# Cross-attention and gated feed-forward on one core: weight loads moved to SP's ring, first rows of maxima to ACT's, normalisation of q and additions of epsilon to POOL

## The reference

```python
q = (x - mean(x, -1)) / sqrt(var(x, -1) + 1e-5)
for head h (16 rows of q and of ctx):
    s = q_h.T @ ctx_h * 16 ** -0.5            # 256 x 256
    att_h = ctx_h @ softmax(s, -1).T          # 16 x 256
x = x + gamma * att
n = layernorm(x)
out0 = gelu(n @ W0a.T + b0a) @ W0b.T + b0b    # 256 -> 512 -> 256
out1 = relu(n @ W1a.T + b1a) @ W1b.T + b1b
x = x + (out0 if argmax(softmax(n @ Wg.T)) == 0 else out1)
```

## Time and profile before

| what | us |
|---|---|
| median of 3 runs | 257.08 (255.61 to 258.86) |
| the profiled execution | 256.82 |
| its span, first to last instruction | 255.0 |
| PE busy with matmuls | 221.7 (87% of the span) |
| DVE busy | 170.5 (67%) |
| ACT busy | 143.6 (56%) |
| POOL busy | 97.0 (38%) |
| POOL's power of 128x1 (L241), mean of 31 | 0.592 |

### The profile page before, as it was taken

The page is one execution under the profiler, slowest core; times in us unless marked ns, Lnnn a source line. Parts: engine busy times, 40 slices in busy tenths (PEclk is TensorE's granted clock), DMA queues, the critical chain, the costliest instruction groups (busy, mean ns, idle before and its releaser), DMA issues.

```text
span 255.0 us, 5113 instructions
## 1 busy us (share of the span) xinstructions
PE 221.7 (87%) x1968; PEld 171.4 (67%) x1968; DVE 170.5 (67%) x354; ACT 143.6 (56%) x216; POOL 97.0 (38%) x126
## 2 busy tenths in 40 slices
PE   0567926888898999999999999999999999899994
PEld 0434513444476879787878887888778687778883
DVE  2777565698986798878878886988597534523302
ACT  2012323467568748874878488758854986532220
POOL 5492230133794842293239224822441145001000
PEclk9999999959799999999999999999999999999999
DMA  4498999884934448266917691758202000000101
GB/s 165 67 182 143 253 196 186 260 121 114 137 93 85 131 82 186 44 164 84 196 21 178 92 182 18 146 101 123 50 20 64 3 23 3 21 23 0 41 0 42
DMA packets 19563, 25.75 MB, mean 101 GB/s; under 512 B 2644, under 2 KB 13140, under 8 KB 19284
## 3 DMA queue, kind: packets, MB, share of 16 engines
q1 hardware_dynamic: 18024, 22.15, 44.7%
q10 hardware_dynamic: 1516, 3.29, 5.1%
HBM read 11.28 MB, written 2.10 MB: 52 GB/s over the span
## 4 chain that ended last, share of the span: by engine, by line
PE 71%; DVE 10%; ACT 8%; DMA 5%; issue 4%; POOL 0%; DVEq 0%; ACTq 0%
PE ff L769 17%; PE od L712 9%; PE ff L790 9%; PE st L700 9%; PE ff L796 5%; PE ff L808 5%; PE smax L688 5%; ACT P L538 4%; DMA qkst<-mlow 3%; PE od L720 3%; DVE nmax L375 3%; PE st L675 2%; ACT hid L578 2%; PE od L727 2%; DVE nmax L368 2%
## 5 line engine op out<-in xcount | busy, mean ns | idle before, releaser
L538 ACT ACTIVATE P<-st 128x1024 f32<-128x1024 f32 x64 | 65.7, 1027 | 58.4 <-PE st L700 49.9
L375 DVE TENSOR_REDUCE nmax<-smax 128x4 f32<-128x1024 f32 x54 | 66.1, 1225 | 28.5 <-PE smax L688 28.1
L241 POOL TENSOR_TENSOR mv<-mv,power 128x1 f32<-128x1 f32 x31 | 18.4, 592 | 73.7 <-DVE mv L340 73.7
L700 PE MATMUL st<-qkst 50*128 50x256 f32 x240 | 31.3, 340 | 13.2 <-ACT P L538 6.7
L769 PE MATMUL ff<-xnTh,w1h 128*128 128x256 f32 x128 | 37.5, 293 | 1.2 <-DVE y L446 1.2
L700 PEld LDWEIGHTS st<-qkst 50*128 50x128 f32 x240 | 18.7, 193 | 27.9 <-ACT P L538 10.2
L578 ACT ACTIVATE hid<-ff,b1t 128x256 f32<-128x256 f32 x64 | 26.8, 471 | 16.7 <-PE ff L769 16.5
L769 PE MATMUL ff<-xnTh,w1l 128*128 128x256 f32 x128 | 36.0, 281 | 0.0
L769 PE MATMUL ff<-xnTl,w1h 128*128 128x256 f32 x128 | 35.9, 281 | 0.0
L265 POOL TENSOR_TENSOR hidL<-hid,hidH 128x1024 fp32r<-128x1024 f32 x12 | 28.6, 2387 | 18.5 <-DVE hidH L435 14.1
L712 PE MATMUL od<-P,vt 128*32 128x256 f32 x512 | 35.5, 424 | 0.0
(11 more groups left out here) (84 smaller groups left out, 353.4 us busy)
## 6 DMA issues: line engine op xcount, KB each, us to landing
qkst<-parts SPq DMA_DIRECT2D x87, 128.0 KB, 4.5
xv<-in_xv SPq DMA_DIRECT2D x16, 256.0 KB, 3.0
qk<-in_qk SPq DMA_DIRECT2D x15, 256.0 KB, 4.0
out<-y SPq DMA_DIRECT2D x16, 128.0 KB, 2.4
w1t<-in_w ACTq DMA_DIRECT2D x1, 1024.0 KB, 10.0
w2t<-in_w ACTq DMA_DIRECT2D x1, 1024.0 KB, 9.0
qkst<-parts ACTq DMA_DIRECT2D x3, 128.0 KB, 6.3
qk<-in_first SPq DMA_DIRECT2D x1, 256.0 KB, 3.9
```

The lines of the kernel that those rows point to most:

```text
L241: pool.tensor_tensor(mv[:, b % 2, 11:12], mv[:, b % 2, 10:11], power[:, 0:1], ALU.pow).then_inc(s_rstd, 1)
L375: dve.tensor_reduce(nmax[:, c % 2, :, :, j].rearrange("p a e -> p e a"), (ff if c in WIDE and j % 2 else smax)[:, :, :, :], AX.X, ALU.max, ...
L538: act.activation(P[:, b % 2, j, :, :, :].rearrange("p e a l -> p (e a l)"), st[:, :, :, :].rearrange("p e a l -> p (e a l)"), ACT.Exp, sca ...
L700: mm = pe.matmul(st[:, e, a, :], qkst[rows, s, j, 1, a * 128:(a + 1) * 128], qkst[rows, s, j, 0, :], start=True, stop=True)
```

## The change

- SP: of the DMAs at the start, `stacks(2)` and `load_qk(4)` come ahead of `load_xv(0)`, and `load_xv(1)` and `load_qk(5)` come behind `stacks(3)`; in b = 1 `load_qk(6)` comes behind `stacks(4)`. `w1t` is loaded by SP at the end of b = 1, `w2t` at the end of b = 2; before, ACT issued them in slots 0 and 4.
- The rows of maxima of samples 1 to 3 are issued by ACT, in its ring, behind `copy_max`; those of samples 4 to 15 stay with SP.
- `q_norm` for samples 2 to 15 runs on POOL, directly behind `rstd`; that of samples 0 and 1 stays on DVE.
- The addition of epsilon moves from DVE to POOL, inside `rstd`, with a semaphore of its own between it and the power.
- ACT makes `w1h` in slots 12 and 13 (before: 8 and 9) and `w2h` in slots 14 and 15 (before: 12 and 13). POOL makes `w1l` in slots 13 and 14 (before: 12 and 13) and `w2l` in slots 16 and 17 (before: 14 and 15).

```diff
+        def max_rows(eng, c):
+            s = place(c, 4)
+            for n, part in enumerate((mhigh, mlow)):
+                eng.wait_ge((s_mhi, s_mrow)[n], c)
+                eng.dma_start(qkst[STACK + n:STACK + n + 65:64, s, :, 0, :].bitcast(F32),
+                             part[:, c % 2, :].bitcast(F32)).then_inc(s_mst[s], 16)
...
+            stacks(2)
+            load_qk(4)
             load_xv(0)
-            stacks(2)
-            load_xv(1)
-            load_qk(4)
             for b in range(B):
-                if b + 5 < B:
+                if b + 5 < B and b >= 2:
                     load_qk(b + 5)
                 if b + 3 < B:
                     stacks(b + 3)
-                if b + 1 < B:
-                    max_rows(b + 1)
+                if b < 2:
+                    load_qk(b + 5)
+                if b == 0:
+                    load_xv(1)
+                if 3 <= b < B - 1:
+                    max_rows(sp, b + 1)
                 if b + 2 < B:
                     load_xv(b + 2)
+                if b == 1:
+                    sp.dma_start(w1t[:, :, :, :].rearrange("p a e f -> p (a e f)"), w1).then_inc(s_w1, 16)
+                if b == 2:
+                    sp.dma_start(w2t[:, :, :].rearrange("p u l -> p (u l)"), w2).then_inc(s_w2, 16)
...
-            def rstd(b, mv, count, s_var, s_rstd):
+            def rstd(b, mv, count, s_var, s_eps, s_rstd):
                 pool.wait_ge(s_var, count)
-                pool.tensor_tensor(mv[:, b % 2, 11:12], mv[:, b % 2, 10:11], power[:, 0:1], ALU.pow).then_inc(s_rstd, 1)
+                m = mv[:, b % 2, :]
+                pool.tensor_scalar_add(m[:, 10:11], m[:, 9:10], EPS).then_inc(s_eps, 1)
+                pool.wait_ge(s_eps, count)
+                pool.tensor_tensor(m[:, 11:12], m[:, 10:11], power[:, 0:1], ALU.pow).then_inc(s_rstd, 1)
+
+            def q_norm(c):
+                m, q = mv1[:, c % 2, :], qk[:, place(c, QK), 0, :]
+                pool.wait_ge(s_rstd1, c)
+                pool.tensor_scalar(q, q, m[:, 8:9], m[:, 11:12], ALU.subtract, ALU.mult).then_inc(s_qn, 1)
...
-            rstd(2, mv1, 2, s_var1, s_rstd1)
-            pool.wait_ge(s_rstd1, 2)
+            rstd(2, mv1, 2, s_var1, s_eps1, s_rstd1)
+            q_norm(2)
+            pool.wait_ge(s_qn, 2)
             pool.wait_ge(s_lo, 1)
             ones_rows(0, slice(1, 4), 3)
             ones_rows(1, slice(1, 4), 4)
...
                 for c in prepared(n):
                     if c > 2:
-                        rstd(c, mv1, c, s_var1, s_rstd1)
+                        rstd(c, mv1, c, s_var1, s_eps1, s_rstd1)
+                        q_norm(c)
...
-                if b == 3 and j >= 2:
-                    pool.wait_ge(s_w2h, j - 1)
-                    half = slice((j - 2) * HM, (j - 1) * HM)
+                if b == 4 and j < 2:
+                    pool.wait_ge(s_w2h, j + 1)
+                    half = slice(j * HM, (j + 1) * HM)
                     pool.tensor_tensor(w2l[:, half, :], ...)
-                if b == 3 and j < LC:
-                    pool.wait_ge(s_w1h, j + 1)
-                    pool.tensor_tensor(w1l[:, j, :, :], ...)
+                if b == 3 and j >= 1 and j <= LC:
+                    pool.wait_ge(s_w1h, j)
+                    pool.tensor_tensor(w1l[:, j - 1, :, :], ...)
...
                 dve.bn_stats(m[:, 0:6], src).then_inc(s_stat, 1)
                 dve.wait_ge(s_stat, count)
-                dve.bn_aggr(m[:, 8:10], m[:, 0:6]).then_inc(s_aggr, 1)
-                dve.wait_ge(s_aggr, count)
-                dve.tensor_scalar_add(m[:, 10:11], m[:, 9:10], EPS).then_inc(s_var, 1)
+                dve.bn_aggr(m[:, 8:10], m[:, 0:6]).then_inc(s_var, 1)
...
                 for p in prepared(n):
                     moments1(p)
-                for p in prepared(n - 1):
-                    q_norm(p)
...
-                if n == 0:
-                    act.dma_start(w1t[:, :, :, :].rearrange("p a e f -> p (a e f)"), w1).then_inc(s_w1, 16)
-                if n == PAIRS:
-                    act.dma_start(w2t[:, :, :].rearrange("p u l -> p (u l)"), w2).then_inc(s_w2, 16)
-                if b == 2 and j < LC:
+                if b == 3 and j < LC:
                     act.wait_ge(s_w1, 16)
                     act.activation(w1h[:, j, :, :], w1t[:, j, :, :], ACT.Copy).then_inc(s_w1h, 1)
-                if b == 3 and j < 2:
+                if b == 3 and j >= 2:
                     act.wait_ge(s_w2, 16)
-                    half = slice(j * HM, (j + 1) * HM)
+                    half = slice((j - 2) * HM, (j - 1) * HM)
                     act.activation(w2h[:, half, :], w2t[:, half, :], ACT.Copy).then_inc(s_w2h, 1)
...
                 if k == 0 and 2 <= c <= B:
                     copy_max(c - 1)
+
+                    if c <= 4:
+                        max_rows(act, c - 1)
```

More of the change, by code:

```diff
@@ L134, in build @@
             sem, ("s_const", "s_ones", "s_kones", "s_bias", "s_wgd", "s_vones"))
[L135 removed]
+        s_stat1, s_var1, s_rstd1, s_qn = map(sem, ("s_stat1", "s_var1", "s_rstd1", "s_qn"))
         s_hi, s_lo, s_k1hi, s_k1lo = map(sem, ("s_hi", "s_lo", "s_k1hi", "s_k1lo"))
         s_x0, s_c0, s_ones0, s_one0, s_m0, s_mrow0 = map(sem, ("s_x0", "s_c0", "s_ones0", "s_one0", "s_m0", "s_mrow0"))
[L138 removed]
+        s_stat0, s_var0, s_rstd0, s_qn0 = map(sem, ("s_stat0", "s_var0", "s_rstd0", "s_qn0"))
+        s_eps0, s_eps1, s_eps2 = map(sem, ("s_eps0", "s_eps1", "s_eps2"))
         s_smax, s_max, s_mT, s_mhi, s_mrow = map(sem, ("s_smax", "s_max", "s_mT", "s_mhi", "s_mrow"))
@@ L190, in stacks @@
                         stack_copy(sp, c, e, r)
-            def max_rows(c):
-                s = place(c, 4)
-                for n, part in enumerate((mhigh, mlow)):
-                    sp.wait_ge((s_mhi, s_mrow)[n], c)
-                    sp.dma_start(qkst[STACK + n:STACK + n + 65:64, s, :, 0, :].bitcast(F32),
-                                 part[:, c % 2, :].bitcast(F32)).then_inc(s_mst[s], 16)
             def store(b):
@@ L282, in _ @@
                                base=0, pattern=[[-1, 128]], channel_multiplier=1).then_inc(s_const, 1)
-            pool.wait_ge(s_var0, 1)
+            pool.wait_ge(s_var0, 2)
+            pool.tensor_scalar_add(mv0[:, :, 10], mv0[:, :, 9], EPS).then_inc(s_eps0, 1)
+            pool.wait_ge(s_eps0, 1)
             pool.tensor_tensor(mv0[:, :, 11], mv0[:, :, 10], power[:, :], ALU.pow).then_inc(s_rstd0, 1)
@@ L286, in _ @@
             pool.tensor_tensor(parts[:, 1, 3, :], qk[:, 0, 1, :], parts[:, 1, 2, :], ALU.subtract).then_inc(s_k1lo, 1)
-            rstd(1, mv1, 1, s_var1, s_rstd1)
+            rstd(1, mv1, 1, s_var1, s_eps1, s_rstd1)
             pool.wait_ge(s_hi, 1)
             pool.tensor_tensor(parts[:, 1, 0, :], qk[:, 0, 0, :], parts[:, 1, 1, :], ALU.subtract).then_inc(s_lo, 1)
-            rstd(2, mv1, 2, s_var1, s_rstd1)
-            pool.wait_ge(s_rstd1, 2)
+            rstd(2, mv1, 2, s_var1, s_eps1, s_rstd1)
+            q_norm(2)
+            pool.wait_ge(s_qn, 2)
             pool.wait_ge(s_lo, 1)
@@ L316, in _ @@
                 if j == 0 and b >= 2:
-                    rstd(b - 2, mv2, b - 1, s_var2, s_rstd2)
+                    rstd(b - 2, mv2, b - 1, s_var2, s_eps2, s_rstd2)
                 if j == 2 and b >= 2:
                     masks(b - 2)
-                if b == 3 and j >= 2:
-                    pool.wait_ge(s_w2h, j - 1)
-                    half = slice((j - 2) * HM, (j - 1) * HM)
+                if b == 4 and j < 2:
+                    pool.wait_ge(s_w2h, j + 1)
+                    half = slice(j * HM, (j + 1) * HM)
                     pool.tensor_tensor(w2l[:, half, :], w2t[:, half, :], w2h[:, half, :], ALU.subtract).then_inc(s_w2l, 1)
-                if b == 3 and j < LC:
-                    pool.wait_ge(s_w1h, j + 1)
-                    pool.tensor_tensor(w1l[:, j, :, :], w1t[:, j, :, :], w1h[:, j, :, :], ALU.subtract).then_inc(s_w1l, 1)
-            rstd(B - 2, mv2, B - 1, s_var2, s_rstd2)
+                if b == 3 and j >= 1 and j <= LC:
+                    pool.wait_ge(s_w1h, j)
+                    pool.tensor_tensor(w1l[:, j - 1, :, :], w1t[:, j - 1, :, :], w1h[:, j - 1, :, :], ALU.subtract).then_inc(s_w1l, 1)
+            rstd(B - 2, mv2, B - 1, s_var2, s_eps2, s_rstd2)
             masks(B - 2)
-            rstd(B - 1, mv2, B, s_var2, s_rstd2)
+            rstd(B - 1, mv2, B, s_var2, s_eps2, s_rstd2)
             masks(B - 1)
@@ L333, in _, with moments @@
         def _(dve):
-            def moments(b, src, mv, count, s_stat, s_aggr, s_var):
+            def moments(b, src, mv, count, s_stat, s_var):
                 m = mv[:, b % 2, :]
@@ L358, in moments1, with q_norm1 @@
                 dve.wait_ge(s_qk[place(c, QK)], 16 * turn(c, QK))
-                moments(c, qk[:, place(c, QK), 0, :], mv1, c, s_stat1, s_aggr1, s_var1)
-            def q_norm(c):
-                m, q = mv1[:, c % 2, :], qk[:, place(c, QK), 0, :]
```

(9 more changed lines are left out.)

8 lines of the change are left out of this document (2 added, 6 removed).

## The result

| | before | after |
|---|---|---|
| median, four runs of each on one chip | 256.67 us | 261.44 us |
| ratio, with its 95% interval | | 1.0165 [1.0108, 1.0221] |
| the profiled execution / its span | 256.82 / 255.0 | 261.95 / 259.3 |
| first scores of sample 1 (wait for `mlow`) | 39.84 | 39.45 |
| transpositions of the maxima of samples 2, 3, 4 | 42.91, 54.21, 64.51 | 42.52, 52.82, 65.17 |

The forecast was 251.8 us, and 261.4 lies outside its range. The milestones (us from the start of the span) place the loss. Sample 1 begins 0.4 earlier, where 6 to 7 us were expected. Between the transpositions of samples 3 and 4 the new kernel takes 12.35 us where the old took 10.30. The first `gemm1` is 2.7 late, the first `low_pass` 4.4 late, and the span is 4.3 longer: behind `low_pass` nothing more changes.

What follows compares the result with a forecast made beforehand. PE bounds the steady stretch (24.18 of 24.60 us busy); earlier it waits, longest from 33.4 to 39.8 for `mlow`. 6.1 + 0.3 - 1.3 + 0.2 = 5.3 off the 255.0 span gave 251.8 us, range 248.5 to 255.5.

Steps and rivals of the forecast that it cites:

- The start: First maxima, without the normalisation on DVE, begin at 15.15 instead of 16.32; 1.0 us gain booked, bounds 0.6 and 1.2.
- The stall at 33.4: PE's wait for `mlow` to 39.8 ends early; transposition of sample 2 from 42.9 to 36.8, 6.1 us gained including the start.
- a late end at 33.4: Row of sample 1 if SP's ring holds it up: 39.8 - 1.0 less 5.4 us for 1 MB, about 33.4.
- I cost this at nothing: `q_norm(2)` ahead of POOL's memsets delays `low(2)` and the last four copies of `stacks(2)`; no loss booked.
- Rival 3: DMAs still bind: `stacks(3)` lands at 36 to 38, or `w1t` delays `stacks(5)`; 1.5 to 3 us back, chance 0.12.
- Should the DMA bind after all, each us past 36 is a us lost: At the stall of sample 1, a DMA landing after 36 us would cost its delay past 36 one for one.
- `q_norm` on POOL: Each normalisation moved from DVE to POOL was taken to last 0.5 us, near a copy of its shape; ends 0.22 and 2.36.
- Rival 4: `q_norm` on POOL is slow: the 5.3 us gain is gone at 3.8 us each, 259.5 at 5; chance 0.04.
- Slots 14 to 16: Moved weight splits on ACT and POOL make the first `gemm1` late; 1.3 us loss booked, low 0.5, high 2.
- Rival 1: The clock falls before the first `gemm1`, doubling the time of its first twelve matmuls: +1.6, 253.4 us, chance 0.2.
- Samples 2 and 3: At 49.10 the normalisation on DVE, 0.40, leaves the chain: 0.3 us gained.
- the end: Additions of epsilon leave DVE ahead of the `y` that the last samples' `gemm1` waits for: 0.2 us gained once.

Runs made afterwards that it cites:

- h1: The kernel before, with only `q_norm` of samples 2 to 15 moved to POOL; 255.48 us, ratio 0.9946.
- g2: g1 with half the rows of ones filled ahead of `rstd(2)` on POOL, half behind `q_norm(2)`, and `low(2)` ahead of filling `vt`; 254.12 us, ratio 0.9886.
- e2: The changed kernel with the splits of the weights back in their slots of before, loads still late; 258.19 us, ratio 1.0047.
- e3: The changed kernel with `q_norm` of samples 2 to 15 back on DVE, a slot later; epsilon stays on POOL; 260.25 us, ratio 1.0152.
- e1: The changed kernel with the rows of maxima of samples 1 to 3 issued by SP again; 257.14 us, ratio 1.0004.
- f6: The changed kernel, rows still in ACT's ring, but SP waits for the exponential before them, restoring the order of issue of e1; 257.31 us, ratio 1.0029.
- f8: The changed kernel with e1, e2 and e3 together (rows, splits and `q_norm` put back); 256.24 us, ratio 0.995.
- g1: f7 with SP issuing the rows of sample 1 ahead of `qk(5)` and `xv(1)` too; 257.14 us, ratio 0.9993.
- e4: The changed kernel with SP holding back `qk(5)`, `xv(1)`, `xv(2)` until the rows of sample 1 have landed; 259.44 us, ratio 1.0074.
- f5: The changed kernel with `stacks(3)` held back as well as the loads e4 holds, until the rows of sample 1 have landed; 260.7 us, one execution.
- f7: The changed kernel with e1 and e2 together (rows back to SP, splits in their slots of before); 253.78 us, ratio 0.9857.
- g3: g2 with `w2t` loaded right behind `w1t`, at the end of b = 1; 253.22 us, ratio 0.987.

## Why the prediction was wrong

**The start (1.0 booked): half right.** The first maxima came as worked out: 15.30 in the timeline of after, where 15.15 was forecast and the earlier trace rows had 16.32. The row of `mrow0` was issued 1.01 earlier (17.69 against 18.70). But `scores0`, which waits for that row, came only 0.43 earlier (20.14 against 20.57): from issue to use the row took 2.45 us, and 1.87 before.

```profile
8.67 0.41 DVE L380 TENSOR_SCALAR qk<-qk,mv 128x256 f32<-128x256 f32 x1 [0.47 <-POOL mv L252]
15.30 1.23 DVE L384 TENSOR_REDUCE nmax<-st 128x4 f32<-128x1024 f32 x1 [0.43 <-PE st L674]
17.93 0.80 PE L701 MATMUL smax<-qkst 48*128 48x256 f32 x4 [0.68 <-DMA qkst<-parts]
20.14 2.08 PE L688 MATMUL st<-qk 17*128 17x256 f32 x8 [0.98 <-issue]
```

Epsilon on POOL puts `q_norm1` 0.67 later (8.67 against 8.00), and with it the stack copies of sample 1 (first issued at 9.64 against 8.97), for which `maxima(1, 0)` now waits, and the loads behind them. h1, where only `q_norm` moved and epsilon stayed on DVE, shows the price: its row is issued at 17.65, as in after, and `scores0` starts at 19.53, 1.88 later. So `q_norm` gave the 1.0 that was booked, and epsilon on POOL took back 0.6. The prediction named both parts ("it lies ahead of the first stack copies", "meets a busier ring") but took only 0.2 off for them (1.0 of 1.17).

**The stall at 33.4: the step that failed.** The prediction took 5.1 us of gain here, besides the start, and 0 came. It failed in three places.

1. *It priced the transfer by the ring it stands in.* Both of its estimates, 32.2 to 33.8 without SP's ring and 33.4 with it, are wrong; the row landed at 39.4. What decides is what was issued before, on either ring. The second row of sample 1, issued between 30.7 and 31.4 (in g2 at 29.8), and its first user on PE:

| kernel | ring of the row | issued before it and not landed | first copy of `stacks(2)` issued | first user |
|---|---|---|---|---|
| before | SP | `stacks(3)`, `w1t` (other ring) | 19.93 | 39.84 |
| after | ACT | `stacks(3)`, `qk(5)`, `xv(1)`, `xv(2)` | 19.68 | 39.45 |
| e2 | ACT | the same | 19.68 | 39.14 |
| e3 | ACT | the same | 18.86 | 38.21 |
| e1 | SP | `stacks(3)`, `qk(5)`, `xv(1)` | 19.62 | 37.84 |
| f6 | ACT | the same | 19.63 | 37.86 |
| f8 | SP | the same | 18.75 | 36.96 |
| g1 | SP | `stacks(3)` | 19.51 | 36.26 |
| e4 | ACT | `stacks(3)` | 19.66 | 36.24 |
| g2 | SP | `stacks(3)` | 17.39 | 33.91 |
| f5 | ACT | nothing | 19.59 | 33.03 |

Two pairs with one order and different rings agree within 0.02 us (e1 and f6, g1 and e4). Each 256 KB taken from ahead of the row gives 0.8 to 1.6. The prediction weighed two statements of the Trainium skill (DMA: Bandwidth & Descriptors, Queues, rings and completion order). By the one, each DMA engine takes turns between rings, and a small transfer on a ring of its own should pass: no run shows it passing. By the other, a completion's increment lands only after every earlier write of that engine, across queues: every line of the table agrees with it. The prediction took it for a late end at 33.4, by subtracting `w1t` (5.4 us at the pace of the stretch) from the old landing. It set nothing against that, and three things belong there. `xv(2)`, which stood behind the row, now stands ahead of it: 1.6 us, by e1. (`qk(5)` and `xv(1)` stood ahead before too, but ahead of `stacks(3)`, and had landed.) `q_norm(2)` on POOL delays `stacks(2)`: 1.2 us, by e3 against after, and 0.9, by f8 against f7. The prediction named this and wrote "I cost this at nothing". And 5.4 is too much for `w1t`: by the pages of before and after, ACT's queue took 5.1% and 2.2% of the 16 engines' time, 13.0 and 5.7 us, which puts each of the two weight tensors at 3.6 us, an estimate. 3.6 less 1.6 less 1.2 leaves 0.8 us of gain; 0.4 was measured.

2. *It did not see what SP's waiting was for.* `max_rows` in SP's stream was also a gate: nothing behind it could start before the maxima were ready. The prediction listed what is late with the weights ("`w2t` likewise. Nothing booked") by when the weights are wanted, and not by whom they overtake. In b = 2 `w2t` goes 0.07 us ahead of the row of sample 3, which then takes 7.46 us, and PE waits 2.50. Rival 3 ("the DMAs still bind") had the right mechanism and put `stacks(3)` at 36 to 38, near where it landed, but named it as the transfer that binds, priced it at 1.5 to 3 us, and had a chance of only 0.12. e1 and f6 show that the gate is worth 4.3 and 4.1 us.

3. *"Should the DMA bind after all, each us past 36 is a us lost" had the limit too late.* PE takes its work in order, and the last maxima of sample 2 stand behind `scores(1, 0)`. The transposition follows the first scores of sample 1 by 3.07 or 3.08 us in before, after, e1, e4, g1 and g2 alike (36.26 to 39.33 in g1, 33.91 to 36.98 in g2). So 36.8 wants the first scores by about 33.7, and each us past that is lost: with the row in use at 36.24 (e4) the transposition comes at 39.32. No run shows whether DVE's own work would hold it at 36.8 with an earlier row. And `stacks(3)` had not landed at 32 to 33, as estimated: with nothing but `stacks(3)` ahead the row lands at 36.2 (e4, g1), and in after its copies take up to 7.5 us from issues that end at 29.3.

**`q_norm` on POOL (0.5 taken, bounds 0.22 and 2.36): 1.24.** The groups of after on POOL, and the columns of the earlier trace rows:

```profile
L257 POOL TENSOR_SCALAR qk<-qk,mv 128x256 f32<-128x256 f32 x14 | 17.4, 1241 | 1.5
L250 POOL TENSOR_SCALAR mv<-mv 128x1 f32<-128x1 f32 x31 | 7.6, 247 | 62.7 <-DVE mv L358 62.7
```

Three times the copy of its shape and three times DVE's 0.40; within the bounds, not near the row it was chosen by. The addition took 0.25 and was priced at 0.22. 17.4 + 7.6 is most of the 28.1 us that POOL gained. Rival 4 (slower than before if `q_norm` takes 3.8 us or more) was far off. The direction of the edit's worth was right: h1 gains 1.1, f7 over f8 2.5. The prediction expected this at 0.3, from one row at 49.10; a larger one is the one at f8's 67.98 and, before, at 70.28 in the chain (0.89), one slot from the first `gemm1`. In the changed kernel nothing of it is left: e3, with `q_norm` back on DVE, is no slower than after. The rule that GpSimd shares its SBUF interfaces with VectorE (the Trainium skill, GPSIMD Engine Reference, 8. Key points) shows in single rows: `high_gelu` on DVE took 2.41 us at 86.51 beside `w2l`, where its median is 0.67. It does not decide the sum.

**Slots 14 to 16 (1.3 booked, 0.5 to 2): mechanism right, too small.** The transposition of sample 4's maxima to the first `gemm1` took 8.80 before and 10.84 after: 2.04 lost by this step where 1.3 was booked, by the two conditions that were named. ACT's two halves of `w2h` put DVE's `xnTl` at 75.65, and POOL's chain ends last:

```profile
73.55 2.36 POOL L346 TENSOR_TENSOR w1l<-w1t,w1h 128x1024 fp32r<-128x1024 f32 x1
```

It ends at 75.91, 0.10 ahead of `gemm1`, where 74.3 was forecast: sample 7's moments came at 68.1 instead of 67.2, and `q_norm` took 1.24 instead of 0.5. In e2 the step takes 8.29. Rival 1 (the clock falls before the first `gemm1`, +1.6, chance 0.2) came true: 0.50 in the window from 76.0. It did so in all six kernels that have the splits in the slots of after (after, e1, e3, e4, f5, f6). And the prediction stopped at `gemm1`: "from there PE is the bound and keeps it". From `gemm1` to `low_pass` another 1.74 went (15.96 against 14.22), by the low clock and by POOL, whose second `w2l`, moved to slot 17 and behind a `q_norm` of 1.24, holds `low_hidden` until 89.55. Two kernels show the clock's part by itself: g1 and g2 have `w2l` in its old slots and the low clock, and take 15.46 and 15.37 from `gemm1` to `low_pass`; e2, f7, f8, g3 and h1, at the high clock, take 14.21 to 14.23. That is 1.2 us for the clock, and leaves about 0.5 for POOL, an estimate. Together the slots cost 3.2 us in e2, more than twice the term.

**Samples 2 and 3 (0.3), the end (0.2).** From the transposition of sample 2 to that of sample 3 the new kernel took 10.30 where the old took 11.30: 1.0 gained. From `low_pass` to the end of the span it took 167.3 against 167.5, which agrees with the 0.2 of the end; a difference this small is shown by one execution of each.

**The sum as it came**, in the span: start and stall 0.39 gained, samples 2 and 3 1.00 gained, rows of sample 3 2.05 lost, slots 2.04 and 1.74 lost, the end 0.1 gained: 4.3 lost. Predicted was 5.3 gained. Two figures of the prediction don't follow from its own terms, and neither decides anything: half of the forecast's chance of 0.49 is 0.245 and not 0.27, and its bounds (0.4 and 0.2 at the start, 0.7 and 0.8 in the slots, 0.6 once) give 250.8 to 253.5 and not 250 to 253.3.

## What to carry to other kernels

A wait in a queue's stream also guards everything behind it; when a step with a wait is moved to another queue, list what the old queue will now issue earlier, and whether that goes ahead of something small that an engine waits for. Price a small DMA by the bytes issued before it on all rings that haven't landed, not by its own ring, and ask what delays those: a step of 1.24 us moved ahead of their source on POOL came back as about 1 us at the small one's user. And where a stretch moves as many bytes as its time holds, taking one wait out of it hands the wait on to the next transfer: gain comes from taking bytes out of the stretch or from starting it earlier (g2), not from its order.
